# Layer 1 of a graph kernel: two harmonics of a piece on even and odd partitions, spread by transfers of step two

## The chip, the cores and the metric

The kernel runs on one NeuronCore of a Trainium2 chip. The metric is the device time of one launch in microseconds (us). Engines: TensorE (PE; PEld is its weight load), VectorE (DVE), ScalarE (ACT), GpSimd (POOL) and SyncE (SP), which here only issues transfers. Sixteen DMA engines carry out the transfers of all of them.

## The reference, cut to what matters

Four graph layers on 3125 nodes and 100000 edges, sorted by destination. The change touches layer 1, and of it the part that forms keys and values of the edges out of the gathered node row and nine spherical harmonics:

```
def tensor_product(x_e, sh, w, C):      # x_e [E,64], sh [E,9], w [E,128], C [64,9,128]
    acc = sh[:, 0:1] * (x_e @ C[:, 0, :])
    for s in range(1, S):
        acc = acc + sh[:, s:s + 1] * (x_e @ C[:, s, :])
    return acc * w
...
k = tensor_product(x_dst, edge_sh, wk, Cqk).reshape(-1, H, DQK)
v = tensor_product(x_dst, edge_sh, wv, Cv).reshape(-1, H, DV)
attn = jnp.einsum('ehd,ehd->eh', q[edge_src], k)
amax = jax.ops.segment_max(attn, edge_src, num_segments=n)
ex = jnp.exp(attn - amax[edge_src])
...
upd = jax.ops.segment_sum(v * alpha[..., None], edge_src, num_segments=n)
```

So for each edge 64 features times 9 harmonics are contracted with a 576 x 256 matrix (keys and values side by side).

## The kernel before, in words

Phases run one after the other, with a barrier between them: for each layer `project` (node tables), `edges_n` (a loop over the edges) and `finish_layer`. Edge j of partition p is edge 784 p + j; a tile t of the loop is 8 such columns on 128 partitions, 1024 edges, and there are NCH = 98 tiles.

`project` of layer 1 turns the node rows X with TensorE, multiplies them by weights, and VectorE adds biases into TAB. SP stores tables: `x1_tab` (x_tab in the profile), 128 wide, is X twice side by side, written by two transfers at the phase's start; `q1_tab` comes out of TAB. POOL meanwhile scatters 25 columns of TAB to `spread_q`.

`edges_1`, for a tile t:
- POOL gathers the 8 columns of node rows from x_tab into G, 512 B a row. Its program is written out in order: four gathers, the product MSG of tile t-4, four gathers.
- TensorE turns G (`turn`) into XT in PSUM: 128 partitions, the 64 features twice, by 1024 edges.
- SP loads SHB, the harmonics spread over partitions: 5 pieces of 1024 columns. A piece k holds harmonic 2k on partitions 0 to 63 and 2k+1 on 64 to 127; each half is one row of HBM repeated for 64 partitions. The ninth harmonic has piece 4 on 64 partitions alone. So there are two transfers, of 5 and of 4 pieces (20480 and 16384 B a partition).
- VectorE multiplies XT by SHB into XF (`outer`: pieces 0 to 3 at L1391, piece 4 on 64 partitions at L1393).
- TensorE (`column`) multiplies each of 8 columns of XF, 5 pieces, by CF (128 x 256 each, fp32), into COLS. The lower half of XF and CF in piece 4 is set to zero once.
- VectorE multiplies COLS by WKV (weights from wkv_tab, keys already times the query Q) into RW, reduces to logits, keeps a running maximum (ARG), and scans the sums (SC); ACT takes exponentials and copies rows out (OUT), which its queue stores.

The order of work is written out by hand. VectorE's step t: product 3 and logits of t-1, `outer` of t+1, sums of t-2, products 0 and 1 of t, the query rows of t+1 (`expand_q`, `ask`), product 2 of t. TensorE's step t: column 0 of t, `turn` of t+1, columns 1 to 7 of t. SP's step t: wait for `outer` of t-2, both SHB transfers of t; wait for product 3 of t-2, WKV of t; wait for `ask` of t-2, Q of t. SHB, XF, G, Q and WKV have two buffers each. `ea9t` (the harmonics) and `cfix` (the matrix) are laid out by the host.

Of the kernel before, what the change touches and what calls it, by code (L numbers as in the profile page):

```python
# [55 lines left out]
def graph_kernel(nc, x, dst_shifted, src, ea16, ea64t, ea9t, etype, ew, w64, we, cfix, w2, b1, b2, wout, vecs, basis,  # L56
# [27 lines left out]
    with top:  # L84
# [113 lines left out]
        with ExitStack() as ctx:  # L198
            def s(name):
                return phase_semaphore(name)  # L200
# [157 lines left out]
        def project(weights, n_out, biases, tables, keep, spread_at=None, spread_tab=spread, width=64, relations=None):  # L358
# [4 lines left out]
            with ExitStack() as ctx:  # L363
# [3 lines left out]
                XT = sb("XT", [64, NPAD], F32, ctx)  # L367
                TAB = sb("TAB", [P, K, n_out], F32, ctx)
                PT = [ctx.enter_context(nc.psum_tensor(unique(f"PT{b}"), [P, 512], F32)) for b in range(2)]
                PO = [ctx.enter_context(nc.psum_tensor(unique(f"PO{b}"), [P, 512], F32)) for b in range(4)]  # L370
# [8 lines left out]
                with nc.Block() as block:  # L379
# [42 lines left out]
                    @block.vector  # L422
                    def _(v):
                        for u, (k0, m) in enumerate(units):
                            v.wait_ge(m_done, u + 1)
                            nc.vector.tensor_tensor(
                                TAB[:, k0:k0 + m, :],
                                PO[u % 4][:, 0:m * n_out].rearrange("p (k n) -> p k n", k=m),
                                biases.unsqueeze(1).to_broadcast([P, m, n_out]), ALU.add).then_inc(m_copied, 1)
# [25 lines left out]
                    def _(sp):  # L455
                        for tab, at, width in tables:
                            if at is None:
                                for copy in range(0, width, 64):
                                    sp.dma_start(tab.rearrange("(p k) f -> p k f", k=K)[:, :, copy:copy + 64],
                                                 X[:, :, :]).then_inc(stored, 16)  # L460
                        if relations is not None:
# [4 lines left out]
                        for ready in (len(units) // 2, len(units)):  # L466
# [5 lines left out]
                            k0 = k1  # L472
                        copies = sum(width // 64 for _, at, width in tables if at is None)
                        sp.wait_ge(stored, 16 * (copies + 2 * len(made)))
                        sp.wait_ge(spread_zeroed, 16 * BLANKS)
# [754 lines left out]
        def edges_1(src_ap):  # L1230

            with ExitStack() as ctx:
# [15 lines left out]
                first_q_in, q_steps, q_expanded = e.sem("first_q_in"), e.sem("q_steps"), e.sem("q_expanded")  # L1248
                w_in, cleared = e.sem("w_in"), e.sem("cleared")
                src_in, flagged, broken = e.sem("src_in"), e.sem("flagged"), e.sem("broken")  # L1250
                asked, weighted = e.sem("asked"), e.sem("weighted")

                with nc.Block() as block:
                    @block.sync
                    def _(sp):
                        sp.dma_start(SRC[:, :], src_ap).then_inc(src_in, 16)
                        for ap, source in ((CF[:, 0:4, :], cfix[0:512, :].rearrange("(k p) n -> p k n", p=P)),
                                           (CF[0:64, 4, :], cfix[512:576, :])):
                            sp.dma_start(ap, source).then_inc(w_in, 16)

                        def step(t, n, b, first, last):
                            if not first:
                                wait(sp, made, t * 2 - 2)
                            sp.dma_start(SHB[b][0:64, :, :].rearrange("p k n -> p (k n)"),
                                         ea9t[bass.ds(t, 1), 0, :].to_broadcast([64, 5 * C * P]))\
                              .then_inc(sh_in[b], 16)
                            sp.dma_start(SHB[b][64:128, 0:4, :].rearrange("p k n -> p (k n)"),
                                         ea9t[bass.ds(t, 1), 1, 0:4 * C * P].to_broadcast([64, 4 * C * P]))\
                              .then_inc(sh_in[b], 16)
                            if not first:  # L1270
                                wait(sp, col_used, t * 4 - 4)
                            sp.dma_start(WKV[b][:, :, :], row_view(wkv_tab, t)).then_inc(wkv_in[b], 16)
                            if not first:
                                wait(sp, q_expanded, t)
                                wait(sp, asked, t - 1)
                            sp.dma_start(Q[b][:, :, :], row_view(spread_q, t)).then_inc(q_in[b], 16)
# [36 lines left out]
                    def _(pe):  # L1313
                        wait(pe, w_in, 16 * 2)
                        wait(pe, cleared, 3)

# [61 lines left out]
                    def _(v):  # L1378
                        nc.vector.memset(CF[64:128, 4, :], 0.0).then_inc(cleared, 1)
                        for b in range(2):  # L1380
                            nc.vector.memset(XF[b][64:128, 4, :], 0.0).then_inc(cleared, 1)
                        e.constants(nc.vector)
                        wait(v, e.ready, e.N_READY)

                        def outer(t, n, b, first):

                            wait(v, sh_in[b], (n + 1) * 32)
                            if not first:
# [3 lines left out]
                                                    SHB[b][:, 0:4, :], ALU.mult).then_inc(made, 1)  # L1392
                            nc.vector.tensor_tensor(XF[b][0:64, 4, :], XT[0:64, :], SHB[b][0:64, 4, :], ALU.mult)\  # L1393
                              .then_inc(made, 1)
# [565 lines left out]
```

## Time and profile before

| | |
|---|---|
| median of 3 runs | 5738.77 us (5714.43 to 5777.18) |
| profiled execution | 5725.51 us |
| its span | 5723.7 us |
| busy: PE, DVE, POOL, ACT | 2880.7, 3771.3, 3692.5, 1703.3 us |
| moved by DMA | 1038.57 MB, 181 GB/s over the span |

The span is the time from the first to the last instruction on the core; some 1.8 us of the execution lie around it. A busy time is the sum over an engine's instructions of the program. The layer-1 edge loop is the stretch from about 1338 to 3300 us, slices 10 to 23 of the page's 40.

### The profile page before, as it was taken

Reading aid. Unit: us, or ns where it says so; the run is one execution under the profiler, and the core shown is the slowest. Engines: PE = TensorE matmul, PEld = TensorE weight load, DVE = VectorE, ACT = ScalarE, POOL = GpSimd, SP = SyncE. Lnnn points to the kernel's source line nnn. Section 1 sums busy time; section 2 is a strip of 40 time slices with the busy share of each in tenths; the row PEclk is TensorE's granted clock in tenths of the full one; section 3 lists DMA queues with packets and bytes.
Section 4 is the critical chain, followed back from the end, with each engine's and each line's share of the span. In section 5 each row is a group of like instructions: output and inputs, shape, how many; then the busy total and the mean of one; then the engine's idle time right before and its main releaser. Section 6 shows DMA issues by size and latency. Waiting matters only on the chain. (4 is left out here: it accounts for less than half of the span.)

```text
span 5723.7 us, 49870 instructions
## 1 busy us (share of the span) xinstructions
PE 2880.7 (50%) x12451; PEld 2294.2 (40%) x12451; DVE 3771.3 (66%) x5980; ACT 1703.3 (30%) x2882; POOL 3692.5 (65%) x3483
## 2 busy tenths in 40 slices
PE   0777777755988999999999950000000530000001
PEld 0444444434877888888888740000000430000000
DVE  3788888865878989898989845656666532222223
ACT  0666666641212222222222212222222321111111
POOL 4777777745655666676766437777777237777775
PEclk8889998867999999999999955555555775555555
DMA  7777777747999999999999733333333452222221
GB/s 265 239 252 257 252 250 248 251 147 187 269 225 243 268 259 254 261 266 261 265 263 267 204 85 103 109 107 107 108 107 102 186 224 54 54 54 54 54 55 44
DMA packets 385790, 1038.57 MB, mean 181 GB/s; under 512 B 145511, under 2 KB 168547, under 8 KB 344613
## 3 DMA queue, kind: packets, MB, share of 16 engines
q1 hardware_dynamic: 221412, 727.15, 44.1%
q0 software_dynamic: 107840, 167.64, 12.6%
q10 hardware_dynamic: 56448, 142.93, 6.8%
q14 instruction: 75, 0.61, 0.0%
q8 instruction: 15, 0.25, 0.0%
HBM read 645.72 MB, written 391.75 MB: 181 GB/s over the span
## 5 line engine op out<-in xcount | busy, mean ns | idle before, releaser
L1336 PE MATMUL COLS<-CF,XF 128*128 128x256 f32 x7840 | 1718.2, 381 | 11.7 <-DVE XF L1393 11.7
L1336 PEld LDWEIGHTS COLS<-CF,XF 128*128 128x128 f32 x7840 | 1489.2, 191 | 212.3 <-DVE XF L1393 12.1
L1304 POOL DMA_INDIRECT G<-x_tab,SRC x784 | 943.1, 1203 | 307.4 <-issue 277.2
L880 ACT ACTIVATE OUT<-SC 128x544 f32<-128x544 f32 (+2 forms) x392 | 553.9, 1413 | 1697.5 <-DVE SC L828 912.8
L1578 PE MATMUL CP<-IDENT,LROW 128*68 128x128 f32 (+1 forms) x12 | 3.4, 421 | 2040.7 <-DVE SM L1699 2040.7
L761 POOL DMA_INDIRECT G<-rel_tab,IDX_rel x784 | 739.6, 943 | 390.4 <-issue 249.2
L761 POOL DMA_INDIRECT G<-xl_tab,IDX_src x784 | 763.7, 974 | 307.4 <-issue 256.8
L761 POOL DMA_INDIRECT G<-kv_tab,IDX_src x784 | 739.7, 943 | 250.7 <-issue 249.6
L1578 PEld LDWEIGHTS CP<-IDENT,LROW 128*68 128x68 f32 (+1 forms) x12 | 1.5, 157 | 2042.3 <-DVE SM L1699 2042.2
L821 DVE TENSOR_TENSOR MSG<-G,EW 128x512 f32<-128x512 f32 x98 | 100.0, 1020 | 733.8 <-DMA G<-rel_tab,IDX_rel 724.7
L1292 POOL TENSOR_TENSOR MSG<-RW,EX 128x1024 f32<-128x1024 f32 x98 | 281.6, 2874 | 422.9 <-DVE ARG L793 419.8
L1391 DVE TENSOR_TENSOR XF<-XT,SHB 128x4096 f32<-128x4096 f32 x98 | 433.6, 4425 | 113.8 <-PE XT L1322 96.7
L998 PE MATMUL WK<-W,HT 128*128 128x256 f32 x1568 | 473.0, 431 | 0.0
L994 PE MATMUL WK<-B2R,ONER 128*128 128x512 f32 x392 | 239.9, 612 | 254.5 <-ACT WKV L1060 254.5
L998 PEld LDWEIGHTS WK<-W,HT 128*128 128x128 f32 x1568 | 343.3, 219 | 59.8
L1415 DVE SCALAR_TENSOR_TENSOR Q<-Q,SAME_HERE 128x128 f32<-128x128 f32 x783 | 274.8, 351 | 26.1 <-DMA Q<-spread_q 1.8
L1060 ACT ACTIVATE WKV<-WK 128x512 f32<-128x512 f32 x392 | 222.4, 595 | 228.4 <-PE WK L998 223.9
L848 ACT ACTIVATE EX<-ARG 128x64 f32<-128x64 f32 (+1 forms) x196 | 55.0, 281 | 778.9 <-DVE ARG L793 778.7
L1402 DVE TENSOR_TENSOR RW<-COLS,WKV 128x512 f32<-128x512 f32 x392 | 259.6, 687 | 38.8 <-PE COLS L1336 23.9
L828 DVE TENSOR_TENSOR_SCAN SC<-DEC,MSG 128x612 f32<-128x612 f32 (+1 forms) x196 | 272.7, 1391 | 14.9
L1452 DVE TENSOR_TENSOR_SCAN SC<-DEC,MSG 128x1224 f32<-128x1224 f32 x98 | 265.5, 2709 | 21.7 <-DVE MSG L1446 9.1
L1166 DVE TENSOR_TENSOR T<-G,XE 128x512 f32<-128x512 f32 x98 | 67.4, 688 | 307.9 <-DMA G<-kv_tab,IDX_src 307.9
(254 smaller groups left out, 4655.8 us busy)
## 6 DMA issues: line engine op xcount, KB each, us to landing
SHB<-ea9t SPq DMA_DIRECT2D x98, 1280.0 KB, 14.7
wkv_tab<-WKV SPq DMA_DIRECT2D x98, 1024.0 KB, 4.3
SHB<-ea9t SPq DMA_DIRECT2D x98, 1024.0 KB, 19.3
WKV<-wkv_tab SPq DMA_DIRECT2D x98, 1024.0 KB, 6.4
scan<-OUT ACTq DMA_DIRECT2D x196, 288.0 KB, 2.6
scan<-OUT ACTq DMA_DIRECT2D x98, 576.0 KB, 8.4
rel_tab<-YS SPq DMA_DIRECT2D x25, 2048.0 KB, 7.4
RAW<-spread SPq DMA_DIRECT2D x196, 256.0 KB
```

The source lines that it names most:

```text
L761: pool.indirect_dma_start(out=self.G[g][b][:, c, :], out_offset=None, in_=tab, in_offset=bass.IndirectOffsetOnAxis(ap=self.IDX[which][b][: ...
L828: nc.vector.tensor_tensor_scan(flat(SC[b][:, 0:R, :]), flat(self.DEC[b][:, :, :]), flat(self.MSG[:, :, :]), 0.0, ALU.mult, ALU.add)\
L880: nc.scalar.activation(self.OUT[b][:, :, 0:R], SC[b][:, 0:R, 1:1 + C].rearrange("p r j -> p j r"), ACT.Copy).then_inc(self.copied_out, 1)
L994: nc.tensor.matmul(WK[cc % 2][:, :], ONER[:, :], B2R[:, :, :].rearrange("p a n -> p (a n)"), start=True, stop=False)
L998: last = nc.tensor.matmul(WK[cc % 2][:, a * 256:(a + 1) * 256], HT[b][:, a, cc * P:(cc + 1) * P], W2[:, :], start=False, stop=(a == 1))
L1292: nc.gpsimd.tensor_tensor(e.MSG[:, 0:128, 1:1 + C].rearrange("p (h c) j -> p h c j", c=CH), RW[b][:, :, 128:256].rearrange("p j (h c) -> p ...
L1304: pool.indirect_dma_start(out=e.G[0][b][:, col, :], out_offset=None, in_=x1_tab, in_offset=bass.IndirectOffsetOnAxis(ap=SRC[:, at:at + 1], ...
L1336: last = nc.tensor.matmul(acc, XF[b][:, k, edges_], CF[:, k, :], start=(k == 0), stop=(k == 4))
L1391: nc.vector.tensor_tensor(XF[b][:, 0:4, :], XT[:, :].unsqueeze(1).to_broadcast([P, 4, C * P]), SHB[b][:, 0:4, :], ALU.mult).then_inc(made, 1)
L1402: nc.vector.tensor_tensor(RW[b][:, two, :], COLS[which][:, :].rearrange("p (c n) -> p c n", c=2), WKV[b][:, two, :], ALU.mult).then_inc(co ...
L1415: ins = nc.vector.scalar_tensor_tensor(out=Q[b][:, j, :], in0=row, scalar=SAME_HERE[b][:, j:j + 1], in1=Q[b][:, j, :], op0=ALU.mult, op1=A ...
L1452: nc.vector.tensor_tensor_scan(flat(SC[b][:, :, :]), flat(e.DEC[b][:, :, :]), flat(e.MSG[:, :, :]), 0.0, ALU.mult, ALU.add)\
```

## The change

- `cfix` is laid out anew: row 2f + a of a piece is feature f of harmonic 2k + a, with a block of zeros for the tenth harmonic, and is loaded by one transfer of all 5 pieces.
- SHB: harmonic 2k goes to the even partitions, 2k+1 to the odd ones, by two transfers whose partitions step by two (`h:P:2`). Both carry 5 pieces; the source row `ea9t` already held zeros for the tenth harmonic.
- x_tab holds every element twice in a row (x0 x0 x1 x1 ...) in place of the row twice. VectorE makes this in XD at the start of `project`, and one transfer stores it.
- XF of piece 4 is formed on all 128 partitions; the three memsets and the semaphore `cleared` go.

```diff
@@ project @@
+                doubles = [tab for tab, at, _ in tables if at is None]
+                if doubles:
+                    XD = sb("XD", [P, K * D, 2], F32, ctx)
+                    doubled = s("doubled")
...
                     @block.vector
                     def _(v):
+                        if doubles:
+                            nc.vector.tensor_copy(XD[:, :, :], X[:, :, :].rearrange("p k f -> p (k f)").unsqueeze(2)
+                                                  .to_broadcast([P, K * D, 2])).then_inc(doubled, 1)
...
-                        for tab, at, width in tables:
-                            if at is None:
-                                for copy in range(0, width, 64):
-                                    sp.dma_start(tab.rearrange("(p k) f -> p k f", k=K)[:, :, copy:copy + 64],
-                                                 X[:, :, :]).then_inc(stored, 16)
+                        for tab in doubles:
+                            sp.wait_ge(doubled, 1)
+                            sp.dma_start(tab.rearrange("(p k) f -> p (k f)", k=K),
+                                         XD[:, :, :].rearrange("p n a -> p (n a)")).then_inc(stored, 16)
...
@@ edges_1, SP @@
-                        for ap, source in ((CF[:, 0:4, :], cfix[0:512, :].rearrange("(k p) n -> p k n", p=P)),
-                                           (CF[0:64, 4, :], cfix[512:576, :])):
-                            sp.dma_start(ap, source).then_inc(w_in, 16)
+                        sp.dma_start(CF[:, :, :], cfix.rearrange("(k p) n -> p k n", p=P)).then_inc(w_in, 16)
...
-                            sp.dma_start(SHB[b][0:64, :, :].rearrange("p k n -> p (k n)"),
-                                         ea9t[bass.ds(t, 1), 0, :].to_broadcast([64, 5 * C * P]))\
-                              .then_inc(sh_in[b], 16)
-                            sp.dma_start(SHB[b][64:128, 0:4, :].rearrange("p k n -> p (k n)"),
-                                         ea9t[bass.ds(t, 1), 1, 0:4 * C * P].to_broadcast([64, 4 * C * P]))\
-                              .then_inc(sh_in[b], 16)
+                            for h in range(2):
+                                sp.dma_start(SHB[b][h:P:2, :, :].rearrange("p k n -> p (k n)"),
+                                             ea9t[bass.ds(t, 1), h, :].to_broadcast([64, 5 * C * P]))\
+                                  .then_inc(sh_in[b], 16)
@@ edges_1, VectorE @@
-                        nc.vector.memset(CF[64:128, 4, :], 0.0).then_inc(cleared, 1)
-                        for b in range(2):
-                            nc.vector.memset(XF[b][64:128, 4, :], 0.0).then_inc(cleared, 1)
...
-                            nc.vector.tensor_tensor(XF[b][0:64, 4, :], XT[0:64, :], SHB[b][0:64, 4, :], ALU.mult)\
+                            nc.vector.tensor_tensor(XF[b][:, 4, :], XT[:, :], SHB[b][:, 4, :], ALU.mult)\
                               .then_inc(made, 1)
@@ host @@
+    def paired(c):
+        return np.concatenate([c, np.zeros((1, 64, 256), f32)]).reshape(5, 2, 64, 256).transpose(0, 2, 1, 3).reshape(5 * P, 256)
```

What SP issues from the start of `project` of layer 1 into the first tile of the edge loop, before:

```order
L459 DMA x_tab<-X 3200x1x64 x2
L470 DMA q_tab<-TAB 128x12x128
L470 DMA q_tab<-TAB 128x13x128
...
L1256 DMA SRC<-src 128x784
L1259 DMA CF<-cfix 128x4x256
L1259 DMA CF<-cfix 64x256
L1264 DMA SHB<-ea9t 64x5120
L1267 DMA SHB<-ea9t 64x4096
L1272 DMA WKV_2<-wkv_tab 128x2048
L1276 DMA Q<-spread_q 128x1024
```

And with the change:

```order
L465 DMA x_tab<-XD 128x3200
L476 DMA q_tab<-TAB 128x12x128
L476 DMA q_tab<-TAB 128x13x128
...
L1261 DMA SRC<-src 128x784
L1262 DMA CF<-cfix 128x5x256
L1268 DMA SHB<-ea9t 64x5120 x2
L1273 DMA WKV_2<-wkv_tab 128x2048
L1277 DMA Q<-spread_q 128x1024
```

The order of the four loads of a tile stays (SHB, SHB, WKV, Q); the second SHB transfer grows from 4096 to 5120 columns, and x_tab goes out in one piece of long rows.

VectorE at the same place, from the last instruction of layer 0 to the first `outer`, before:

```order
L1869 TENSOR_TENSOR X<-SQ,SN 125x1600
...
L426 TENSOR_TENSOR TAB<-PO_3,VEC 128x384 x2
...
L432 COPY KEEP<-TAB 128x1600
...
L1379 MEMSET CF 64x256
L1381 MEMSET XF 64x1024 x2
L695 MEMSET SC 128x1224
...
L1415 SCALAR_TENSOR_TENSOR Q<-FIRST_Q,SAME_HERE,Q 128x128
...
L1391 TENSOR_TENSOR XF<-XT,SHB 128x4096
L1393 TENSOR_TENSOR XF<-XT,SHB 64x1024
```

And with the change:

```order
L1866 TENSOR_TENSOR X<-SQ,SN 125x1600
...
L429 COPY XD<-X 128x3200
L433 TENSOR_TENSOR TAB<-PO_3,VEC 128x384 x2
...
L439 COPY KEEP<-TAB 128x1600
...
L700 MEMSET SC 128x1224
...
L1412 SCALAR_TENSOR_TENSOR Q<-FIRST_Q,SAME_HERE,Q 128x128
...
L1388 TENSOR_TENSOR XF<-XT,SHB 128x4096
L1390 TENSOR_TENSOR XF<-XT,SHB 128x1024
```

A copy of 3200 elements a partition now stands ahead of TAB, three memsets are gone, and the second product of `outer` covers 128 partitions. TensorE and POOL issue the same instructions in the same order.

## Rows read from the trace of the kernel before

**Rows 1.** The page's 40 slices of the span (143 us each).

```profile
PE   0777777755988999999999950000000530000001
...
PEclk8889998867999999999999955555555775555555
DMA  7777777747999999999999733333333452222221
```

**Rows 2.** Stretches: length, busy us of PE, PEld, DVE, ACT, POOL, PEclk, DMA share, GB/s.

```profile
1378.00:3231.00 1853.00, 1753.03 (x8369) 1524.44 (x8368) 1642.63 (x2274) 388.65 (x658) 1183.69 (x850) 0.99 1.00 258
...
2486.70:2504.90 18.20, 18.20 (x89) 16.01 (x89) 17.11 (x24) 4.15 (x7) 13.14 (x9) 1.00 1.01 271
2504.90:2523.25 18.35, 18.31 (x90) 15.89 (x89) 17.35 (x26) 4.14 (x7) 12.77 (x9) 1.00 1.02 271
```

**Rows 3.** All instances of the first product of `outer`, L1391.

```profile
L1391 DVE TENSOR_TENSOR XF<-XT,SHB x98: 4419/4425/4426, 1368.1 to 3250.4; 128x4096 f32<-128x4096 f32 x98
```

**Rows 4.** Waits from 1360 to 3300 us: total us, times, longest.

```profile
POOL G L1304 <- issue: 273.0, 705, 17.0
...
PE XT L1322 <- DMA G<-x_tab,SRC: 152.6, 76, 52.3
```

**Rows 5.** DMA issues of 2000 to 3200 us: KB each, median us to landing.

```profile
SHB<-ea9t SPq DMA_DIRECT2D x62, 1280.0 KB, 14.6
WKV<-wkv_tab SPq DMA_DIRECT2D x62, 1024.0 KB, 6.2
SHB<-ea9t SPq DMA_DIRECT2D x62, 1024.0 KB, 19.1
scan<-OUT ACTq DMA_DIRECT2D x62, 576.0 KB, 8.2
Q<-spread_q SPq DMA_DIRECT2D x62, 512.0 KB, 8.4
```

**Rows 6.** DMA, 2505.5 to 2509 us: WKV and Q of a tile, 128 partitions.

```profile
DMA packets 238, 1.34 MB, mean 382 GB/s; under 512 B 31, under 2 KB 31, under 8 KB 119
```

**Rows 7.** DMA, 2510 to 2516 us: SHB of the same tile, 64 partitions.

```profile
DMA packets 70, 1.16 MB, mean 193 GB/s; under 512 B 11, under 2 KB 11, under 8 KB 11
```

**Rows 8.** DMA, 3392 to 3401 us: BASIS, 64 partitions, rows not repeated.

```profile
DMA packets 129, 1.85 MB, mean 206 GB/s; under 512 B 16, under 2 KB 16, under 8 KB 16
```

**Rows 9.** DMA, 10.4 to 12 us: mostly VEC, one row repeated for 128 partitions.

```profile
DMA packets 113, 0.44 MB, mean 277 GB/s; under 512 B 34, under 2 KB 34, under 8 KB 113
```

**Rows 10.** Timeline of one tile: start us, us, engine, line, out<-in.

```profile
2521.80 0.33 SPq L1272 DMA_DIRECT2D WKV<-wkv_tab  x1
...
2523.44 0.59 SPq L1267 DMA_DIRECT2D SHB<-ea9t  x1
...
2534.23 0.94 POOL L1304 DMA_INDIRECT G<-x_tab,SRC  x1 [0.30 <-issue]
...
2537.99 1.71 POOL L1304 DMA_INDIRECT G<-x_tab,SRC  x1 [0.30 <-issue]
...
2542.36 1.09 PE L1322 MATMUL XT<-IDENT,G 128*128 128x128 f32 x8 [0.75 <-DMA G<-x_tab,SRC]
```

**Rows 11.** Timeline of `project` of layer 1 and the loop's first tile.

```profile
1293.96 3.76 SPq L459 DMA_DIRECT2D x_tab<-X  x2
...
1300.38 7.97 DVE L426 TENSOR_TENSOR TAB<-PO,VEC 128x384 f32<-128x384 f32 x13 [7.33 <-PE PO L394]
...
1308.39 1.82 DVE L432 COPY KEEP<-TAB 128x1600 f32<-128x1600 f32 x1
...
1332.74 0.98 POOL L448 DMA_INDIRECT spread_q<-TAB,START_AT  x1 [0.31 <-issue]
...
1339.57 0.91 DVE L1381 MEMSET XF<- 64x1024 f32 x1 [0.16 <-issue]
...
1363.81 0.35 DVE L1415 SCALAR_TENSOR_TENSOR Q<-FIRST_Q,SAME_HERE,Q 128x128 f32<-128x128 f32 x1 [19.06 <-DMA Q<-spread_q]
```

**Rows 12.** `outer`'s second product over all tiles, mean ns and idle time before it.

```profile
L1393 DVE TENSOR_TENSOR XF<-XT,SHB 64x1024 f32<-64x1024 f32 x98 | 118.1, 1205 | 0.0
```

## What the change was predicted to do

> **What bounds the kernel now.** Begin with the page's 40 slices [rows 1]. The change acts in layer 1's edge loop, slices 10 to 23. There TensorE stands at 9 tenths or more, and so do the 16 DMA engines: two resources are full at once, which no other stretch shows. Next, which of them ends last. The window over nearly the whole loop [rows 2] gives TensorE 1753.03 busy of 1853 us at a granted clock of 0.99, so it idles 100.0 us, and DMA a share of 1.00 at 258 GB/s. VectorE has 1642.63 us, 89%, POOL 64%. The 98 products of `outer` start from 1368.1 to 3250.4 us [rows 3]: 1882.3 / 97 = 19.41 us a tile. Single tiles show the floor [rows 2]: in 18.20 and 18.35 us TensorE is busy throughout. That floor is some 90 matrix instructions a tile, which the change doesn't touch. So a tile costs 1.1 us more than TensorE needs, some 110 us over the loop; by TensorE's own idle time it is 100.
>
> The table of waits says what that time is [rows 4]: TensorE's transposes wait 152.6 us, 76 times, for the gathers of G; 52.3 of it is the loop's first wait, 100.3 the other 75. Nothing else holds TensorE there. Why are gathers late? In the timeline of one tile [rows 10] SP issues WKV, Q and both SHB transfers between 2521.80 and 2524.0. POOL has issued the last of that tile's gathers a long way back: columns 4 to 7 of a tile come before the four that end with the issue at 2537.99, thus before 2534.23, and the transpose still waits until 2542.36, 8 us. In the issue table [rows 5] a burst of four loads lands after 6.2 (WKV), 8.4 (Q), 14.6 and 19.1 us (SHB, SHB). 19.1 us is the whole period: the DMA engines work through one burst just as the next arrives, and gathers, issued meanwhile, get through slowly between the long rows of SHB. The loop is bound by TensorE with the DMA engines so close behind that most tiles lose 1 to 2 us to them.
>
> **What the DMA engines do in a tile.** Two windows of one burst differ by a factor of two. WKV and Q, 128 partitions, flow at 382 GB/s [rows 6]. SHB, each half on 64 neighbouring partitions, flows at 193 [rows 7]. Is it the 64 partitions, or that one row of HBM is read 64 times? BASIS, 64 partitions with a row each of its own, has 206 GB/s [rows 8]; VEC, one row repeated on all 128 partitions, 277 [rows 9]. So the half is mostly due to the 64 neighbouring partitions, and repeating a row costs some too. The sum by tile, in us: SHB 2304 KB = 2.36 MB at 193 GB/s, 12.2; WKV and Q 1.57 MB at 382, 4.1; OUT and the gathers 576 + 512 KB = 1.11 MB, taken at 382, 2.9. Together 19.2, beside 19.41 measured.
>
> **The change, part by part.**
> *SHB on even and odd partitions.* Bytes grow to 2560 KB = 2.62 MB, by 0.26 MB. No row of the trace shows transfers of step two, so their rate is bounded by neighbours: 193 GB/s if 64 partitions are what counts, 382 if the spread over all 128 is what counts and repeating costs nothing. SHB then takes 13.6 or 6.9 us, the tile's DMA sum 20.6 or 13.9. I take 277, the row that is nearest in kind (a repeated row, spread over all partitions): 9.5 us, sum 16.5, 1.8 us below TensorE's floor of 18.3. Two break points follow. At 215 GB/s SHB takes 12.2 us as now and nothing changes; from 232 on (11.3 us) the sum is under 18.3, and TensorE alone bounds the loop. Above 232 the exact rate is worth nothing more.
>
> What is late next when gathers come in time? VectorE: 17.11 to 17.35 us busy in the full tiles [rows 2], a gap of 1 us. POOL: 12.77 to 13.14 us busy, at 1.25 us a gather [rows 10]. So the floor is TensorE's 18.3. Of 100 us idle I let 80 go. One piece I leave in is the longest POOL pause of the loop, 17.0 us of "issue" [rows 4], for which the trace names no releaser; the rest is ripple. Gain 80.
>
> The Trainium skill bears on this in the page "SBUF — State Buffer", section "Door 1: The DMA port swizzle": a partition's number selects one of 16 ports, partitions 0 to 63 reach 8 of them, and bandwidth goes with the ports reached. This trace agrees as far as it goes: 193 and 206 against 382 GB/s. Even partitions touch all 16 ports by that rule; an estimate by its 436 GB/s would be 6.0 us for SHB, which gives the same time as 277, since TensorE bounds either way.
>
> *First tiles.* The first Q is waited for until 1363.81 [rows 11], behind CF, SHB and WKV in SP's queue. CF grows by 64 KB (0.2 us); SHB falls from 12.2 to 9.5 us: gain 2.5 us (at 193 GB/s: a loss of 1.6).
>
> *Second product of `outer`.* 64 to 128 partitions at 1024 elements each, 1205 ns [rows 12]. L1391 takes 4425 for 4096 elements on 128 partitions [rows 3], 1.08 ns an element; L1393 has 1.18 with 64. Time goes by elements, not partitions: 0. At worst VectorE's slack of 1 us a tile covers it.
>
> *Memsets.* Three go, 0.91 us for each of the XF pair [rows 11] and a quarter of the elements for CF, about 2 in all. VectorE waits 19.06 us for Q afterwards: 0.
>
> *The doubled rows.* One copy of 3200 elements. KEEP's copy of 1600 took 1.82 us [rows 11]; twice that is 3.6. It starts at about 1294.0, as SP does, and ends near 1297.7, ahead of TAB at 1300.38: hidden by the transposes, 0; without that cover 3.6. x_tab's store (1600 KB) now waits for it: at 382 GB/s 4.3 us; at half of that, 8.6, it lands by 1307. POOL's last scatter is issued at 1332.74 [rows 11], and the phase waits for that. 0. SP's next store waits for TAB anyway. Gathers read 512 B a row as before, and matmuls have the same shapes.
>
> Sum against the profiled 5725.5 us (span 5723.7): -80 - 2.5 = 5643. The three runs' median, 5738.8, lies 13 above that execution; on its scale 5656.
>
> **The rivals.**
> *A, above: gathers in time.* For it: rows 6 to 9, and that 232 of a possible 382 GB/s is enough.
>
> *B, slower: step two flows as 64 neighbours do.* The 16 DMA engines share out 64 rows a transfer, as for BASIS; if the limit is how these rows meet at the partitions' side at one time rather than which partitions are named, the rate stays 193 to 206 and only bytes are added: 0.26 MB at 193, 1.36 us a tile, at 206, 1.27. The DMA sum, 20.6, then bounds the loop outright: 98 x 1.3 = +127, and 5866. It decides below 215 GB/s. Against it: a rate that hits exactly the old value needs the engines to keep meeting in step, while gathers and OUT stores push them apart. This is also the case in which the change doesn't do what it says. A rule of the Trainium skill speaks for it, in "DMA: Bandwidth & Descriptors", "Rules for kernel authors": two transfers to disjoint partition halves are no gain, one of 128 partitions is wanted. Read strictly, two transfers of 64 partitions stay two, and the time is this rival's; no row here shows such a pair of step two.
>
> *C, within 1%: between the break points.* At 215 to 232 GB/s, or where the waits for gathers have another cause: POOL's own pace (1.25 us a gather, then MSG) doesn't change, and if the landing of a gather is slow of itself, the 100 us stay. Gain 0 to 50, centre 20: 5719. Against it: the 8 us between issue and use, when POOL is done early.
>
> *D: more load lowers TensorE's clock.* The loop runs at 0.99; slices of layer 0 are at 0.8 to 0.9 with TensorE at 7 [rows 1], and no slice is both full and slowed. One per cent of clock costs 17.5 us. I fold it into C.
>
> **How the numbers follow.** A 0.56, B 0.17, C with D 0.27. A's own range is a gain of 50 to 110 us, on the medians' scale 5629 to 5689. The forecast is A's 5656. For 8 in 10 the range leaves out B, most of its 0.17, and little else: from 5622 (all 110 us and the first tiles) to 5765 (C with a slight loss). About 1% is what measurement of this kernel tells from no change, since its three runs spread over 63 us, 1.1%. 1% is 57 us. A lies mostly beyond it (0.50 of its 0.56), C within it: faster 0.51, same 0.32, slower 0.17.
>
> **What the next profile would show.** Right: SHB lands under 16 us, the rate in its windows is above 232 GB/s, the DMA share falls from 1.00 to about 0.9, the wait for G falls from 100 us to some 20, the starts of `outer` are 18.4 to 18.6 us apart, and XD's copy takes 3.6 us and delays nothing. Wrong: SHB's median landing of 20 us or more, a share still at 1.00 and a period near 20.7 (B); or SHB landing early and the wait for G left (C). A copy of several times 3.6 us, or an x_tab store of short pieces, would put the phase before on the path.

## The result, and the profile after

| | before | with the change |
|---|---|---|
| median | 5736.28 us (5714.43 to 5777.18, 4 runs) | 5583.78 us (5583.02 to 5583.90, 4 runs) |
| profiled execution | 5725.51 us | 5583.82 us |
| its span | 5723.7 us | 5582.0 us |

The ratio is 0.9735 [0.9683, 0.9787]: 2.65% faster. The forecast was 5656 us, the range 5622 to 5765; the time lies 38 us below the range. The two profiled executions differ by 141.7 us, and it is this difference that is divided up below.

The page's 40 slices with the change, to be laid beside [rows 1] (140 us each):

```profile
PE   0777777754999999999999640000000620000001
...
PEclk8888989886999999999999755555555865555555
DMA  7777777764777777777777423333333642222221
```

In the loop, TensorE stays at 9 and DMA falls from 9 to 7: of two full resources one is left. The next view puts numbers to it. All instances of the first product of `outer`, then two stretches (length, busy us of PE, PEld, DVE, ACT, POOL, PEclk, DMA share, GB/s), the loop between the same tiles as far as [rows 2] goes, and one tile; the third fence is the same stretch of the kernel before, 1379.10 to 3231.27, cut as exactly to the same 95 tiles.

```profile
L1388 DVE TENSOR_TENSOR XF<-XT,SHB x98: 4417/4424/4426, 1357.9 to 3111.5; 128x4096 f32<-128x4096 f32 x98
```

```profile
1369.76:3093.42 1723.66, 1723.66 (x8362) 1522.73 (x8361) 1629.89 (x2274) 387.84 (x657) 1203.19 (x849) 1.00 0.76 290
2440.28:2458.41 18.13, 18.13 (x90) 16.02 (x89) 17.25 (x24) 4.18 (x8) 12.78 (x9) 1.00 0.77 293
```

```profile
1379.10:3231.27 1852.17, 1752.20 (x8361) 1523.63 (x8360) 1642.63 (x2275) 388.92 (x658) 1183.96 (x850) 0.99 1.00 258
```

TensorE is busy for the whole of 1723.66 us; before it idled 99.97 of 1852.17. And its busy time itself fell, from 1752.20 to 1723.66 us for the same matrix instructions. The DMA share went from 1.00 to 0.76 while GB/s rose from 258 to 290. A tile takes (3111.5 - 1357.9) / 97 = 18.08 us, before 19.41 [rows 3].

The waits of 1300 to 3200 us (total us, times, longest), to be laid beside [rows 4]:

```profile
POOL G L1305 <- issue: 227.1, 727, 2.3
...
PE XT L1322 <- DMA G<-x_tab,SRC: 49.7, 1, 49.7
...
DVE Q L1412 <- DMA Q<-spread_q: 14.2, 1, 14.2
```

Of TensorE's 76 waits for gathers one is left, the loop's first. POOL's longest unexplained pause went from 17.0 to 2.3 us. What the transfers now do: all DMA of 2442.5 to 2450 us, a stretch like that of [rows 7], and of 2000 to 3100 us the issues as in [rows 5] (SHB has no landing in this view).

```profile
DMA packets 327, 3.13 MB, mean 418 GB/s; under 512 B 75, under 2 KB 75, under 8 KB 198
...
q1 hardware_dynamic: 254, 2.96, 93.6%
```

```profile
SHB<-ea9t SPq DMA_DIRECT2D x122, 1280.0 KB
WKV<-wkv_tab SPq DMA_DIRECT2D x61, 1024.0 KB, 5.0
...
Q<-spread_q SPq DMA_DIRECT2D x61, 512.0 KB, 5.9
```

418 GB/s where SHB had 193 [rows 7]; it is even above the 382 of the transfers of 128 partitions [rows 6]. Q lands after 5.9 us instead of 8.4. Last, `project` and the loop's first tile, as in [rows 11]:

```profile
1291.53 1.83 DVE L429 COPY XD<-X 128x3200 f32<-128x3200 f32 x1 [0.96 <-PEq L118]
...
1293.38 0.33 SPq L465 DMA_DIRECT2D x_tab<-XD  x1
...
1297.48 7.97 DVE L433 TENSOR_TENSOR TAB<-PO,VEC 128x384 f32<-128x384 f32 x13 [4.12 <-PE PO L398]
...
1305.49 1.82 DVE L439 COPY KEEP<-TAB 128x1600 f32<-128x1600 f32 x1
...
1335.04 0.35 SPq L1261 DMA_DIRECT2D SRC<-src  x1
...
1347.25 0.94 POOL L1305 DMA_INDIRECT G<-x_tab,SRC  x1 [0.30 <-issue]
...
1353.55 0.35 DVE L1412 SCALAR_TENSOR_TENSOR Q<-FIRST_Q,SAME_HERE,Q 128x128 f32<-128x128 f32 x1 [14.21 <-DMA Q<-spread_q]
...
1354.65 1.94 PE L1322 MATMUL XT<-IDENT,G 128*128 128x128 f32 x8 [49.73 <-DMA G<-x_tab,SRC]
...
1357.86 4.42 DVE L1388 TENSOR_TENSOR XF<-XT,SHB 128x4096 f32<-128x4096 f32 x1
```

TAB and KEEP begin 2.90 us earlier than before, both alike, so the copy and the single store delay nothing (the 2.9 us were there at the phase's start; layer 0 isn't changed). From TAB (1297.48) to the first `outer` it is 60.38 us, before 1368.1 - 1300.38 = 67.7: 7.3 less. Q of the first tile comes 7.3 us sooner after the load of SRC; SHB at 418 in place of 193 GB/s accounts for 5.9 of it (2.36 MB then, 2.62 now), an estimate from these two rates.

**Where the 141.7 us went.** Between first and last `outer` 1882.3 - 1753.6 = 128.7 us: 100.0 of TensorE's idle time, 28.5 of its busy time. Ahead of the loop's first `outer` 10.2: 7.3 of first loads, 2.9 of drift in what isn't changed. After the last one 2473.3 - 2470.5 = 2.8.

Why is TensorE busy for 28.5 us less with the same instructions? Its two groups of instructions in the 95 tiles (count, busy us, mean ns, idle us before them), before and then with the change:

```profile
L1336 PE MATMUL COLS<-CF,XF 128*128 128x256 f32 x7601 | 1664.2, 380 | 0.0
L1322 PE MATMUL XT<-IDENT,G 128*128 128x128 f32 x760 | 105.8, 284 | 100.0 <-DMA G<-x_tab,SRC 99.6
```

```profile
L1336 PE MATMUL COLS<-CF,XF 128*128 128x256 f32 x7602 | 1656.7, 379 | 0.0
L1322 PE MATMUL XT<-IDENT,G 128*128 128x128 f32 x760 | 98.5, 273 | 0.0
```

Two things went. First, neighbouring instructions overlap in the trace: the two groups add up to 1770.0 us before, 17.8 more than the 1752.20 in which any was running, and to 1755.2 with the change, 31.5 more than 1723.66. After a wait there is nothing for the transpose to overlap with, so 13.7 us of overlap were missing. Second, the instructions themselves were longer by 14.8 us. Part of that is the clock. Two stretches of the kernel before, around one late gather, then the longest of the five stretches of its 95 tiles in which the granted clock was at the lower of its two levels (1.2 GHz instead of 2.4), with the sum over all five:

```profile
1612.00:1642.00 30.00, 17.99 (x87) 15.58 (x85) 17.28 (x24) 4.17 (x8) 21.66 (x17) 0.86 1.03 230
1642.00:1664.00 22.00, 22.00 (x98) 19.29 (x99) 17.28 (x25) 2.45 (x3) 3.77 (x4) 0.88 0.57 132
```

```profile
1633.75:1647.41 13.66, 5.57 (x17) 4.80 (x18) 3.57 (x1) 0.61 (x4) 8.29 (x8) 0.50 1.05 226
...
sum 30.73, PE 21.30 PEld 18.20 DVE 15.96 ACT 3.83 POOL 21.62; mean PE 4.26 PEld 3.64 DVE 3.19 ACT 0.77 POOL 4.32
```

TensorE idles 12.0 us up to 1641.84; the clock falls while it is idle, and stays at the lower level for the first 5.6 us of its work. For 21.3 us TensorE was busy at the lower level, where its products for COLS start 427 ns apart instead of 216. So half of the 21.3, 10.7 of the 28.5 us, are clock; with the change, these 95 tiles have no such stretch. The other 17.9 us (28.54 - 10.65), over 75 waits, are 0.24 us a wait: the lost overlap and slightly longer transposes (mean 284 ns, with the change 273). "Two cuts" below agrees, with a granted clock of 1.00 over its 95 tiles: TensorE is busy 18.0 us more than with the change, at 52 waits for gathers.

```profile
1781.18:3553.45 1772.27, 1741.62 (x8361) 1516.97 (x8360) 1641.63 (x2275) 388.13 (x657) 1212.30 (x850) 1.00 1.01 269
```

### The profile page after: what moved, and what is told of

Read it like the earlier page. It is cut to its first block and busy times, and to the rows that moved or that the text cites. A ratio compares the mean times of both kernels' runs of the same rounds, so it can differ in the third digit from the quotient of the medians.

```text
span 5582.0 us, 49866 instructions
## 1 busy us (share of the span) xinstructions
PE 2846.7 (51%) x12451; PEld 2290.8 (41%) x12451; DVE 3756.5 (67%) x5978; ACT 1702.8 (31%) x2882; POOL 3715.1 (67%) x3483
## 5 line engine op out<-in xcount | busy, mean ns | idle before, releaser
L1305 POOL DMA_INDIRECT G<-x_tab,SRC x784 | 963.6, 1229 | 246.1 <-issue 227.1
```

Of the source, the lines that this page charges most:

```text
L1305: pool.indirect_dma_start(out=e.G[0][b][:, col, :], out_offset=None, in_=x1_tab, in_offset=bass.IndirectOffsetOnAxis(ap=SRC[:, at:at + 1], ...
```

## The experiments

Letters in the expectations beyond A to D of the prediction. S: the rate of a transfer depends on how widely its partitions lie, 64 neighbours being slow. S2, used from the second kernel on: what counts is that rows for both halves of the partitions are in flight at the same time, by whatever means. V: short rows are faster of themselves. T: the layout of x_tab, or its store, makes the gathers faster. The first four and the last four kernels ran where layer 0 is slower (the kernel before takes 6316.02 us beside the first, 6382.95 beside the last), the middle four where it takes 5726.0. The loop is hardly touched by that, so its length from first to last `outer` is given each time; beside it stand 1882.3 us (19.41 a tile) before and 1753.6 (18.08) with the change.

**Neighbours again.** The changed kernel with SHB on halves, x_tab's rows and `cfix` to match; copy, single store, 5 pieces each stay.

```diff
-                                sp.dma_start(SHB[b][h:P:2, :, :].rearrange("p k n -> p (k n)"),
+                                sp.dma_start(SHB[b][64 * h:64 * h + 64, :, :].rearrange("p k n -> p (k n)"),
```

> The changed kernel with the step taken back and nothing else: the harmonics on partitions 0 to 63 and 64 to 127, still two transfers of 5 pieces, x_tab still made by one copy and stored by one transfer. Theory S (where the 64 partitions lie sets the rate of a transfer): SHB flows at 193 to 206 GB/s again, with 0.26 MB more than before the change, so a tile's DMA sum is about 20.6 us, the DMA engines bound the loop, DMA share 1.00, and the time is 5584 + 97 x (20.6 - 18.1) = about 5825 us, slower than the kernel before by 60 to 130 us. Rival T (the gain came from the other parts: equal transfers, the table in long rows, no memsets): within 20 us of 5584.

6466.95 us (6437.23 to 6499.04), ratio 1.0212 [1.0149, 1.0275]. All instances of `outer`'s first product, and the waits from 1780 to 3800 us:

```profile
L1388 DVE TENSOR_TENSOR XF<-XT,SHB x98: 4417/4424/4426, 1771.2 to 3801.3; 128x4096 f32<-128x4096 f32 x98
```

```profile
PE XT L1322 <- DMA G<-x_tab,SRC: 192.3, 82, 5.4
...
DVE XF L1388 <- DMA SHB<-ea9t: 73.3, 20, 7.7
```

20.93 us a tile, and besides the gathers SHB itself is late in 20 tiles. It is the time of rival B: of the parts of the change, the stepped partitions alone carry the gain. The rest costs time; the second transfer grows by a quarter, 1.4 us a tile by [rows 7], of the 1.5 measured. The loss of 151 us is a little more than the 60 to 130 expected.

**Halves, piece by piece, alternating.** As the last, but ten transfers of 64 neighbours and one piece each; the order goes lower, upper, lower, upper.

```diff
+                            for k in range(5):
+                                for h in range(2):
+                                    sp.dma_start(SHB[b][64 * h:64 * h + 64, k, :],
+                                                 ea9t[bass.ds(t, 1), h, k * C * P:(k + 1) * C * P]
```

> As e1_neighbours, but the two halves are loaded piece by piece in turn, ten transfers of 64 neighbouring partitions x 4096 B per tile. Theory S1 (a transfer of 64 neighbours is slow by itself, the 16 engines work on the same transfer at the same time): rate about 200 GB/s, time as e1, about 5825 us, plus the cost of eight more issues on SP, which is idle anyway. Theory S2 (what counts is what all engines write at one time, and they drift apart between short transfers of the two halves): rate above 232 GB/s, loop bound by TensorE, time 5584 to 5620 us.

6222.2 us (6214.81 to 6234.78), ratio 0.9842 [0.9788, 0.9897]; loop 1761.9 to 3530.0 = 1768.1 us, 18.23 a tile. No transfer is stepped here, and all but 14.5 us of the loop's gain is there. S as first put (a transfer's own partitions set its rate) can't explain it.

**Step four.** Four transfers of 32 partitions, step four.

```diff
+                            for q in range(4):
+                                sp.dma_start(SHB[b][q:P:4, :, :].rearrange("p k n -> p (k n)"),
+                                             ea9t[bass.ds(t, 1), q % 2, :].to_broadcast([32, 5 * C * P]))
```

> The changed kernel with each SHB transfer cut in two of step four: partitions q, q+4, q+8 ... for q = 0 to 3, 32 rows of 20480 B each, same bytes and layout. Theory S (spread over all 128 partitions gives the full rate): rate stays near 418 GB/s, time within 5 us of 5584. Rival R (64 rows in a transfer are needed, or step four meets at the partitions' side as neighbours do): rate falls to 200 to 300; under 232 GB/s the loop slows and the time goes above 5600, at 209 to about 5720.

6199.39 us (6187.28 to 6222.22), ratio 0.9816 [0.9759, 0.9874]; loop 1753.7 us, as with the change. 32 partitions a transfer are no loss.

**The table alone.** The kernel before with the copy into XD (its layout kept, rows twice) and the single store.

> The kernel before with only the table part of the change: x_tab's row twice made by one VectorE copy of 3200 elements and stored by one transfer of 25600 B rows; harmonics, CF and memsets as before. Theory S: nothing, within 20 us of 5736, period of a tile 19.4 us, since the phase ends with POOL's scatter. Rival T: a part of the 152 us, 30 or more, comes with it.

6322.48 us (10 runs, 6282.27 to 6352.6), ratio 1.0003 [0.9970, 1.0035]; loop 1885.7 us; TensorE still waits 102.2 us, 79 times, for gathers. T falls: the table's layout and store don't make the gathers faster.

**One and two transfers more a tile.** The changed kernel, and behind each tile's SHB one or two transfers of the same source rows (1280 KB) to a scratch table in HBM that nothing reads; shown for one, with `range(2)` for two.

```diff
+                            for h in range(1):
+                                wait(sp, spare_in[h], t * 16)
+                                sp.dma_start(spare[h],
+                                             ea9t[bass.ds(t, 1), h, :].to_broadcast([64, 5 * C * P]))\
+                                  .then_inc(spare_in[h], 16)
```

> The changed kernel with one more transfer in each tile behind SHB: the row of the even harmonics read 64 times and written to a scratch array in HBM that nobody reads, 1.31 MB. By the tile's DMA sum: share 0.76 of 18.14 us = 13.8 us now; 1.31 MB at 418 GB/s is 3.1 us, sum 16.9, below TensorE's 18.14: theory S (a tile costs the larger of DMA sum and TensorE time) says no loss, loop within 10 us of the changed kernel's 1754 us. Rival U (the two overlap badly, gathers come late as soon as the engines have little idle time): 0.5 us a tile or more, 50 us.

> As e4_extra1 with two such transfers, 2.62 MB more per tile. Sum 13.8 + 6.3 = 20.1 us, above 18.14. Theory S: the DMA engines bound the loop at 20.1 to 21 us a tile, 190 to 280 us more than the changed kernel, DMA share 1.00 and waits for G back. Rival: no loss, if the share counts engines as busy that could take more.

With one: 5596.45 us (5591.57 to 5600.32), ratio 0.9770 [0.9737, 0.9803], loop 1752.5 us; 365 GB/s from 2300 to 3100 us, and nothing lost in the loop. With two: 5727.02 us (10 runs, 5723.73 to 5736.82), ratio 0.9997 [0.9971, 1.0024]. That it is just the time of the kernel before is chance. It is 135 us more than the changed kernel run beside it, where 190 to 280 were expected: the loss came, but smaller than the sum put it (19.42 us a tile, not 20.1 to 21). Its view of DMA from 2300 to 3100 us and of `outer`:

```profile
DMA packets 41595, 326.95 MB, mean 409 GB/s; under 512 B 9900, under 2 KB 9900, under 8 KB 25729
...
SHB<-ea9t SPq DMA_DIRECT2D x84, 1280.0 KB, 16.1
spare<-ea9t SPq DMA_DIRECT2D x82, 1280.0 KB, 19.3
```

```profile
L1397 DVE TENSOR_TENSOR XF<-XT,SHB x98: 4416/4425/4426, 1370.0 to 3253.4; 128x4096 f32<-128x4096 f32 x98
```

At 409 GB/s the engines are full (share 1.01), a tile takes 19.42 us, and the wait for gathers is back with 93.1 us, 74 times. So the changed loop has room: at 409 GB/s 18.1 us carry 7.4 MB, and it moves 18.13 x 293 = 5.3. This pair also shows the step of the argument that the change by itself doesn't: filling the DMA engines is enough to bring the waits for gathers back, with nothing else changed. TensorE's extra busy time is back with them: over the 95 tiles 1760.29 us, against 1723.66.

**Halves, pieces in turn.** The ten transfers of "alternating" with the two loops swapped: five of the lower half, then five of the upper.

```diff
-                            for k in range(5):
-                                for h in range(2):
+                            for h in range(2):
+                                for k in range(5):
```

> As e2_alternate, same ten transfers of 64 neighbours x 4096 B, but in another order: five pieces of partitions 0 to 63, then five of 64 to 127. Tells the alternation from the short rows. Theory S2 (engines that have drifted apart write to both halves at once): no alternation, so the rate is back at about 200 GB/s, 20.9 us a tile as e1_neighbours, loop 2030 us. Rival V (short rows of 4096 B are what helped): as e2_alternate, 18.2 us a tile, loop 1768 us.

5985.00, 5892.93, 5888.80 and 5766.88 us: 4% apart, too wide for an interval, all above the 5726.0 of the kernel before, and 175 to 393 us above the changed kernel run beside it. In the profiled one (5985.00) the loop takes 1374.6 to 3518.0 = 2143.4 us, at 237 GB/s. Waits from 1376 to 3515 us:

```profile
DVE XF L1389 <- DMA SHB<-ea9t: 380.7, 92, 6.4
PE XT L1323 <- DMA G<-x_tab,SRC: 55.4, 51, 2.1
```

Same transfers, same bytes, only their order differs from the kernel with 18.23 us a tile. Even the fastest of the four executions is 175 us above the changed kernel, so V falls, and S2 fits. The 22.1 us a tile are those of the slowest execution; if all the difference lies in the loop, the fastest had about 19.9 (an estimate: 1752.9 + 174.6 us over 97 tiles).

**The changed kernel again**, beside the last three.

> The changed kernel again, unaltered, beside the others on their chip, since the first four ran where the kernel before takes 6316 us. All theories: loop of 1754 us as in its first profile, about 130 us shorter than the kernel before's, and the total shorter by 130 to 155 us.

5592.28 us (5591.17 to 5596.50), ratio 0.9762 [0.9730, 0.9795], loop 1752.9 us.

**The kernel before, alternating.** Nothing of the change; SHB in nine transfers of a piece, halves in alternation.

```diff
+                            for k in range(5):
+                                for h in range(2 if k < 4 else 1):
+                                    sp.dma_start(SHB[b][64 * h:64 * h + 64, k, :],
...
```

> The kernel before (old layout, no extra bytes, old table and memsets) with one thing changed: SHB loaded piece by piece, lower and upper half in turn, nine transfers of 64 x 4096 B. Theory S2 (the halves meet less because engines that have drifted apart write to both): as e2_alternate with 0.26 MB less, loop about 1765 us, 18.1 to 18.3 us a tile, total 115 to 130 us under the kernel before, or within 20 us of the changed kernel. Rival W (e2's gain came with the changed kernel's other parts): 19 us a tile or more.

6260.79 us (6258.62 to 6266.08), ratio 0.9813 [0.9772, 0.9855]; loop 1757.1 us, 18.11 a tile, at 278 GB/s. An order of issue gives within 3.5 us of what the new layout gives in the loop. But it gives no such room. All DMA of 2506.5 to 2516 us, most of one tile's SHB:

```profile
DMA packets 767, 2.47 MB, mean 260 GB/s; under 512 B 164, under 2 KB 164, under 8 KB 767
```

260 GB/s, above 193 and not 418, and the DMA share over the loop is 0.99, as before, where step two has 0.76. It is just enough for the gathers to be in time (TensorE waits for them 4 times, 2.7 us in all); what more load would do to it was not tried.

**The kernel before, two cuts.** Four transfers: pieces 0 and 1 of the lower half, of the upper, then the rest of each (rows of 8 and 12 KB, 8 KB for the last).

> As e10_before_alternate with two cuts in place of five: pieces 0 and 1 of the lower half, of the upper half, then the rest of each (rows of 8192, 12288 and 8192 B). Engines in a burst stand up to about 1 us apart, a transfer of 4 rows of 8192 B lasts 1.3 to 2.5 us, one of 4096 B 0.6 to 1.2. Theory S2: less gain than e10, something between, 18.4 to 19.1 us a tile. Rival: all of the gain as soon as the halves alternate at all, 18.2.

6303.36 us (6271.69 to 6339.13), ratio 0.9896 [0.9849, 0.9943]; loop 1802.0 us, 18.58 a tile, 270 GB/s; 27.3 us of waits for gathers, 52 times, and 12.9 for SHB, 13 times. It lies between one cut and five: the coarser the alternation, the less of it.

**Two queues.** The kernel before with the upper half issued from ACT's queue, at the start of ACT's step, and the lower by SP as before.

```diff
+                        def upper(t):
+                            wait(act, made, t * 2 - 2)
+                            act.dma_start(SHB[t % 2][64:128, 0:4, :].rearrange("p k n -> p (k n)"),
...
```

> The kernel before with the upper half of SHB issued from ACT's queue and the lower from SP's, both whole as before, so that each DMA engine has a row of either half at hand. If an engine takes rows from both queues in turn, the halves are written at the same time and the rate rises above 232 GB/s: 18.2 to 18.5 us a tile, total 80 to 130 us under the kernel before (theory S2). Rival X (rows taken in turn bring the engines together again, or OUT's stores behind the upper half come late): no gain, 19.4 us a tile, or a loss if scans wait for OUT.

6523.5 us (6513.71 to 6530.64), ratio 1.0219 [1.0175, 1.0264]; loop 2026.3 us, 20.89 a tile. The forecast from S2 was missed. The timeline of one tile (start us, us, queue, line):

```profile
2516.35 0.33 ACTq L887 DMA_DIRECT2D scan<-OUT  x1
2516.72 0.47 ACTq L1357 DMA_DIRECT2D SHB<-ea9t  x1
...
2520.84 0.33 SPq L1269 DMA_DIRECT2D WKV<-wkv_tab  x1
2521.27 2.72 SPq L1273 DMA_DIRECT2D Q<-spread_q  x1
2524.03 0.47 SPq L1264 DMA_DIRECT2D SHB<-ea9t  x1
2524.83 4.42 DVE L1397 TENSOR_TENSOR XF<-XT,SHB 128x4096 f32<-128x4096 f32 x1 [1.59 <-DMA SHB<-ea9t]
```

The upper half goes out at 2516.72 and the lower 7.3 us later, behind WKV and Q. All DMA of 2519 to 2523 us, of 2523 to 2527.4 and of 2527.6 to 2532, each with its largest queue (q10 is ACT's, q1 SP's):

```profile
DMA packets 54, 0.84 MB, mean 209 GB/s; under 512 B 3, under 2 KB 3, under 8 KB 3
q10 hardware_dynamic: 54, 0.84, 98.0%
...
DMA packets 277, 1.53 MB, mean 347 GB/s; under 512 B 32, under 2 KB 32, under 8 KB 149
q1 hardware_dynamic: 261, 1.53, 93.1%
...
DMA packets 56, 0.98 MB, mean 223 GB/s; under 512 B 8, under 2 KB 8, under 8 KB 8
q1 hardware_dynamic: 56, 0.98, 105.6%
```

First the upper half, then WKV and Q, then the lower half: each half flows at the old rate. The two halves are not under way together, so the edit didn't make S2's condition, and S2 with two queues stays untested. `outer` now waits 275.4 us, 91 times, for SHB. Why it is also slower than the kernel before isn't settled: the lower half is now last of its burst, but no run separates that from what the earlier store and SHB do to each other on ACT's queue.

**Q first.** The changed kernel with the first tile's loads in the order Q, WKV, SHB, SHB, to see what ends last once DMA is free.

> The changed kernel with the loads of the loop's first tile in another order: Q and WKV, then SHB, since VectorE's first work there is on Q, for which it waits 14.2 us. All else as in the changed kernel. Expected by theory S: Q comes 6 to 7 us earlier, the query rows and their product (4.3 us) move ahead of the wait for SHB, the first outer starts 2 to 5 us earlier, loop and the rest unchanged: 5580 to 5588 us where the changed kernel has 5584 to 5592 on the same chip. Rival: the gathers of the first tile end last and nothing is gained.

6239.07 us (6 runs, 6236.12 to 6254.27), ratio 0.9780 [0.9747, 0.9812] to the kernel before; the changed kernel's ratio in other places was 0.9735 and 0.9762. First tile:

```profile
1772.27 0.35 SPq L1261 DMA_DIRECT2D SRC<-src  x1
...
1779.25 0.35 DVE L1417 SCALAR_TENSOR_TENSOR Q<-FIRST_Q,SAME_HERE,Q 128x128 f32<-128x128 f32 x1 [2.70 <-DMA FIRST_Q<-q_tab,FIRST_DST]
...
1784.77 0.94 POOL L1310 DMA_INDIRECT G<-x_tab,SRC  x1 [0.30 <-issue]
...
1793.42 1.94 PE L1327 MATMUL XT<-IDENT,G 128*128 128x128 f32 x8 [51.27 <-issue]
...
1795.47 4.43 DVE L1393 TENSOR_TENSOR XF<-XT,SHB 128x4096 f32<-128x4096 f32 x1 [11.82 <-issue]
```

VectorE no longer waits for Q, and then stands idle 11.82 us: the transpose begins 8.65 us after the issue of the eighth gather, and `outer` 23.2 us after SRC (22.8 with the change as it is). The profile names no releaser for either pause; the transposes have only gathers and CF to wait for, and the eighth gather is issued 12.5 us after SRC, so gathers most likely end last. The expected 2 to 5 us were not gained.

No version's ratio is below the changed kernel's 0.9735. In the loop step four (1753.7 us), one transfer more (1752.5) and the changed kernel again (1752.9) are alike.

S2 is the reading that fits all of these; it was not seen itself, since no view tells which partitions a packet writes.

## Why the prediction was right in kind and 72 us off, outside its range

**The mechanism was right.** Case A, "gathers in time", happened: the DMA share fell below 1, the waits for G went, TensorE alone bounds the loop. What the next profile was to show came out as put for the rate (above 232), the share (0.76, "about 0.9" was too cautious) and the delays (none). The starts of `outer` are 18.08 us apart, less than the 18.4 to 18.6 that were put. Two steps of the sum failed: 20 of the 100 us of idle time were kept back, and TensorE's busy time was taken as fixed.

**The break points held.** By the sum, SHB above 232 GB/s leaves the loop to TensorE, and more is worth nothing. 418 did bring nothing beyond that: the kernel before with alternating transfers has SHB at 260 GB/s, near the 277 of the sum, and needs 18.11 us a tile; and with DMA filled again by two spare transfers the tile went back to 19.42. Rival B's price held too: 1.3 us a tile were named for 5 pieces at the old rate, and the kernel with neighbours took 20.93, 1.5 more than 19.41.

**The terms that were mis-sized**, all in one direction:

- "Of 100 us idle I let 80 go." All 100 went. The 20 that I kept back were POOL's pause of 17.0 us, "for which the trace names no releaser", and ripple. The pause ended at 1613.13 us, 16.7 us ahead of the 12.0 us wait shown above. With the change the longest is 2.3 us. It stays at 14.4 us with the table alone, at 15.5 with neighbours, and is 6.8 where spare transfers fill the engines: it goes with SHB on whole halves; by which way is not shown. 20 us.
- TensorE's 1753 us of busy time, held fixed since the change doesn't touch the "some 90 matrix instructions a tile". The instructions stayed, their time did not: 28.5 us went, the largest term. 10.7 were busy time at the lower clock, 17.9 what the waits cost beside their length, 0.24 us each. Rival D weighed that more load would cost clock; the 0.99 of [rows 2] was to be read the other way round, as idle time that costs clock. No rival had the lost overlap.
- First tiles: 2.5 us predicted, 7.3 measured, for the most part because SHB flows at 418. 4.8 us.
- "+13" to come from the profiled execution to the median. It was scatter between executions of the kernel before, 63 us in four runs; with the change they lie within 0.9 us (5.3 in the second set), and the profiled one is at the median. 13 us.
- Drift in layer 0 and behind the loop, 5.7 us, in no sum.

Together 20 + 28.5 + 4.8 + 13 + 5.7 = 72.0, the distance from 5656 to 5584. The range's low end, "all 110 us and the first tiles", held no term for busy time and kept the 13 us; without both mistakes it would have been 5580.5, and with either one alone it would still lie above the time (5593.5 or 5609). Its words also give 5738.8 - 110 - 2.5 = 5626, not 5622; that changes nothing.

**The copy.** 3.6 us were predicted for XD by doubling KEEP's 1.82; it took 1.83. Both were hidden, so the sum doesn't change, but time didn't go by elements written here: KEEP's copy of 1600 out of TAB takes as long as XD's 3200 out of X.

**The second product of `outer`** was right: 128 partitions by 1024 take 1.21 us as 64 did [rows 12].

**The rule of the Trainium skill** ("DMA: Bandwidth & Descriptors", "Rules for kernel authors", two transfers to disjoint partition halves are no gain) spoke for B. For whole halves, one behind the other, the kernel with neighbours agrees: 20.93 us a tile. For stepped partitions the measurement decides against it, 418 GB/s, and for halves in alternation in part: 260 GB/s for SHB, between 193 and 418, and 18.11 us a tile. The other page, "SBUF — State Buffer", "Door 1: The DMA port swizzle", fits: an estimate by its figure was 6.0 us for SHB; 2.62 MB at 418 GB/s are 6.3.

## What to carry to other kernels

When two transfers fill the two halves of the partitions one after the other, half of the destination stands still each time: step their partitions, which here gave 418 GB/s and room for another transfer, or cut them and alternate the halves, which gave 260 and just sufficed; see in the rate of that window whether it took. Where TensorE bounds a stretch, its waits cost more than their length, so the sum needs a second term for the busy time that comes back: here 0.24 us a wait, and half the busy time at the lower clock. The offset between the profiled execution and the median was scatter of the kernel before: it doesn't carry over to another kernel.

## What was not expected of the hardware

- Alternating transfers to the two halves, from one queue, run the loop at 291 GB/s (18.23 us a tile), the same transfers half by half at 237 (22.1 us in the profiled execution, the slowest). Cut once, 270. A DMA share of 1.00 didn't tell which: before it went with 75 waits for gathers, in the kernel before with alternation 0.99 with 4.
- Repeating one row of HBM for 64 partitions costs nothing visible: 418 GB/s for SHB, in rows of 20 KB. The 277 of VEC [rows 9] was a poor neighbour.
- 12 us without work for TensorE, and the first 5.6 us of work after it ran at the lower clock. Over the loop 100 us of waits went with 28.5 us of extra busy time, 10.7 of it clock.
- The kernel before spreads over 63 us from run to run, the changed one over 0.9. Why is not shown. A full DMA alone doesn't explain it: two spare transfers (share 1.01) give 13 us in ten runs, with 74 waits for gathers. POOL's long pauses go with much of it: the table alone has one of 14.4 us and spreads over 70 us in ten runs. But step four spreads over 35 us in four runs, with a longest pause of 2.3.
